# Softmax attention in a fused two-layer kernel: who empties v and the sums of values, and where the output projections are summed

## What is computed

```python
def _L0_attn_a_ref(x, Wq, Wk, Wv, Wo):          # 16 heads of 16
    q, k, v = (heads(x @ W.T) for W in (Wq, Wk, Wv))
    att = jnp.einsum('bhqd,bhkd->bhqk', q, k) / jnp.sqrt(16)
    p = jax.nn.softmax(att, axis=-1)
    out = jnp.einsum('bhqk,bhkd->bhqd', p, v)
    return merge(out) @ Wo.T

def _L1_attn_b_ref(x, W_q, Wd_kv, W_uv, W_uk, W_o, gamma, beta):   # latent keys and values, causal
    c_kv = _layernorm(x @ Wd_kv.T, gamma, beta)                    # 64 wide
    scores = einsum(q, absorbed_k, c_kv) / np.sqrt(16)             # masked above the diagonal
    v_full = heads(c_kv @ W_uv.T)
    ctx = einsum(softmax(scores), v_full)
    return merge(ctx) @ W_o.T

x = x + _L0_attn_a_ref(_layernorm(x), ...)      # layer 1, "MHA" below
x = x + ...                                     # layers 2 to 6: experts, linear attentions, experts
x = x + _L1_attn_b_ref(_layernorm(x), ...)      # layer 7, "MLA" below
x = x + _L1_ffn_ref(_layernorm(x), ...)         # layer 8
```

## Time and profile before

| | us |
|---|---|
| median of 3 runs (3069.28 to 3079.09) | 3072.86 |
| the profiled execution | 3071.74 |
| its span, first to last instruction | 3070.0 |
| TensorE busy in it, share of the span | 2791.3, 91% |
| VectorE busy | 1616.8, 53% |
| ScalarE busy | 844.4, 28% |
| GpSimd busy | 996.4, 32% |
| mean granted TensorE clock | 0.924 |

### The profile page before, as it was taken

One profiled execution on the slowest core, in us unless ns is written; L12 is line 12 of the kernel. 1 busy time (PEld: TensorE's weight loads), 2 busy tenths in 40 slices (PEclk: granted clock), 3 DMA queues, 4 the chain that ended last, 5 costly groups with the idle time before them and its releaser, 6 DMA issues. The chain is left out here.

```text
span 3070.0 us, 45793 instructions
## 1 busy us (share of the span) xinstructions
PE 2791.3 (91%) x15592; PEld 1943.7 (63%) x15592; DVE 1616.8 (53%) x4517; ACT 844.4 (28%) x1372; POOL 996.4 (32%) x1109
## 2 busy tenths in 40 slices
PE   7999999999999999999978999999999658888876
PEld 3434448887656556788867888888887533443444
DVE  4566645555655647455534333333344566555556
ACT  2343344443111101344432222222222002222210
POOL 0000027766544435577741122222221011212211
PEclk8999999999999999999989999999998558888875
DMA  3000020000000000200000000000000000000000
GB/s 142 1 0 0 0 103 1 0 0 0 1 0 0 0 0 0 83 0 0 0 14 1 15 15 15 15 1 15 15 1 1 24 0 1 1 1 0 1 0 28
DMA packets 6289, 37.96 MB, mean 12 GB/s; under 512 B 273, under 2 KB 4369, under 8 KB 4497
## 3 DMA queue, kind: packets, MB, share of 16 engines
q1 hardware_dynamic: 6160, 36.34, 3.0%
HBM read 34.24 MB, written 2.10 MB: 12 GB/s over the span
## 5 line engine op out<-in xcount | busy, mean ns | idle before, releaser
L603 PE MATMUL banks<-back 32*128 32x512 f32 (+3 forms) x1088 | 363.9, 599 | 31.5 <-DVE back L613 22.3
L365 PE MATMUL banks<-moe_parts 128*128 128x512 f32 x1536 | 366.9, 394 | 16.8 <-POOL moe_parts L471 10.3
L830 ACT ACTIVATE back<-banks 128x1024 f32<-128x1024 f32 (+3 forms) x256 | 217.1, 863 | 457.8 <-PE banks L724 457.5
L365 PEld LDWEIGHTS banks<-moe_parts 128*128 128x128 f32 x1536 | 286.2, 190 | 79.7 <-issue 22.4
L1449 PE MATMUL banks<-lin_parts 128*128 128x512 f32 x1152 | 309.1, 414 | 19.3 <-DVE lin_parts L1705 15.5
L1640 DVE TENSOR_TENSOR ffn_pack<-banks,back 128x512 f32<-128x512 f32 x128 | 88.5, 692 | 393.7 <-PE banks L1462 393.6
L1449 PEld LDWEIGHTS banks<-lin_parts 128*128 128x128 f32 x1152 | 213.2, 194 | 78.2 <-issue 31.2
L724 PE MATMUL banks<-back 32*128 32x512 f32 (+3 forms) x1024 | 239.4, 577 | 20.2 <-DVE back L846 12.8
L603 PEld LDWEIGHTS banks<-back 32*128 32x128 f32 x1088 | 134.2, 197 | 186.3 <-DVE back L617 77.9
L1770 POOL TENSOR_TENSOR ffn_pack<-ffn_pack 128x256 f32<-128x256 f32 x112 | 82.6, 738 | 456.9 <-ACT ffn_pack L1603 455.5
L617 DVE TENSOR_REDUCE back<-banks 128x1 f32<-128x512 f32 x272 | 176.5, 687 | 80.3 <-PE banks L603 75.6
(11 more groups left out here) (234 smaller groups left out, 5154.6 us busy)
## 6 DMA issues: line engine op xcount, KB each, us to landing
back<-p_raw SPq DMA_DIRECT2D x8, 1024.0 KB, 4.8
back<-p SPq DMA_DIRECT2D x1, 7696.0 KB, 21.2
ffn_pack<-ffn SPq DMA_DIRECT2D x1, 6144.0 KB, 26.8
back<-p SPq DMA_DIRECT2D x1, 5152.0 KB, 15.1
back<-p SPq DMA_DIRECT2D x2, 1792.0 KB, 8.2
out<-x SPq DMA_DIRECT2D x1, 2048.0 KB, 7.5
x<-x_in SPq DMA_DIRECT2D x1, 1536.0 KB, 12.7
small_pack<-small SPq DMA_DIRECT2D x1, 619.0 KB, 5.0
```

The costliest lines, as they stand in the source:

```text
L365: mm = nc.tensor.matmul(bank[:], up[:, n % 2, a, which, kd, :], xp[:, b, kd, :], start=((a, b, kd) == (0, 0, 0)), stop=((a, b, kd) == (1, ...
L603: nc.tensor.matmul(bank[:, 0:n], qs[head_rows[j], hg, qi * P:(qi + 1) * P], ks[head_rows[j], hg, 0:n], start=True, stop=True).then_inc(D.f ...
L830: nc.scalar.activation(pt[:, (kt % 2) * 2 + pair, :, q0:T], two[:, :, q0:T], ACT.Exp, scale=0.25).then_inc(A.free.s, 2)
```

## The change

- v: each of the four tiles now has a bank of ring A, and ScalarE copies it into `v` (128 x 256 each), at the start of ScalarE's turn. VectorE's three copies go. TensorE's two waits behind the last v tile go; in their place the transposed scores wait for their own two banks, the first sums of values (in the second key tile) wait for the last v copy, and v tile 2 waits until both adds of the turn before are done (`y_free`), since the banks 2 and 3 hold y.
- Sums of values: ScalarE copies `os_`, behind `keep_qk`, where VectorE did behind `put_max`.
- y: tiles 0 and 1 are summed in bank 2, tiles 2 and 3 in bank 3, and no longer as uses of ring A. Only the first matmul into a bank has the start flag. VectorE makes two adds of 128 x 512, each after both of its tiles; two new semaphores (`y_full`, `y_free`) tie them. TensorE waits for the last `keep_qk` ahead of the first projection, not ahead of the third.

```diff
-V_TILES = ((0, 1), (2,), (3,))
+    y_banks = c.banks[2:4]
-    A.open(HG * (2 + NT * HJ) + NT)
-    D.open(KD + w.extra_uses + len(V_TILES) + HG * (max_uses + 2))
+    A.open(NT + HG * (2 + NT * HJ))
+    D.open(KD + w.extra_uses + HG * (max_uses + 2))
...
+                def v_tile(i):
+                    pe.wait_ge(A.free.s, A.may_fill(it))
+                    w.v(A.fill("v", i)[:, 0:DM], i).then_inc(A.full.s, 1)
...
                 def project(i, groups):
                     for hg in groups:
-                        mm = nc.tensor.matmul(A.banks[A.index["y", i] % 4][:, 0:DM],
+                        mm = nc.tensor.matmul(y_banks[i // 2][:, (i % 2) * DM:(i % 2 + 1) * DM],
                                               os_[:, hg, i * P:(i + 1) * P], w.wo[:, hg, :],
-                                              start=(hg == 0), stop=(hg == HG - 1))
+                                              start=(hg == 0 and i % 2 == 0), stop=(hg == HG - 1),
+                                              skip_group_check=True)
...
-                for tiles in V_TILES:
-                    v_tiles(tiles)
-                pe.wait_ge(D.free.s, D.released(it, "v", V_TILES[-1]))
-                pe.wait_ge(A.free.s, A.all_free(it))
+                for i in range(NT):
+                    if i == 2:
+                        pe.wait_ge(c.y_free.s, c.y_free.at(it, 0))
+                    v_tile(i)
...
+                        if (hg, kt) == (0, 1):
+                            pe.wait_ge(A.free.s, A.released(it, "v", NT - 1))
...
+                pe.wait_ge(A.free.s, A.released(it, "k", 1))
                 for i in range(NT):
-                    pe.wait_ge(A.free.s, A.may_fill(it))
-                    A.fill("y", i)
                     project(i, range(HG - 1))
                 turn_reciprocals(HG - 1)
                 pe.wait_ge(D.free.s, D.released(it, "reciprocals", HG - 1))
                 for i in range(NT):
-                    project(i, range(HG - 1, HG)).then_inc(A.full.s, 1)
-                pe.wait_ge(A.free.s, A.released(it, "k", 1))
+                    mm = project(i, range(HG - 1, HG))
+                    if i % 2:
+                        mm.then_inc(c.y_full.s, 1)
                 pe.wait_ge(D.free.s, D.released(it, "turn", 0))
+            pe.wait_ge(c.y_free.s, c.y_free.at(B, 0))
...
         def _(act):
             with act.Fori(0, B) as it:
+                for i in range(NT):
+                    act.wait_ge(A.full.s, A.may_read(it))
+                    bank = A.read("v", i)
+                    nc.scalar.activation(v[:, i, :, 1:1 + DH], bank[:, 0:DM].rearrange("p (h d) -> p h d", d=DH),
+                                         ACT.Identity).then_inc(A.free.s, 1)
...
                     keep_qk(act, it, (hg + 2) % HG)
+                    act.wait_ge(O.full.s, O.may_read(it))
+                    bank = O.read("o", hg)
+                    nc.scalar.activation(os_[:, hg, :], bank[:], ACT.Identity).then_inc(O.free.s, 1)
...
         def _(dve):
-                for tiles in V_TILES:
-                    keep_v(tiles)
...
-                    dve.wait_ge(O.full.s, O.may_read(it))
-                    bank = O.read("o", hg)
-                    nc.vector.tensor_copy(os_[:, hg, :], bank[:]).then_inc(O.free.s, 1)
                 invert(HG - 1)
                 normalise(HG - 1)
-                for i in range(NT):
-                    n = A.index["y", i]
-                    dve.wait_ge(A.full.s, A.full.at(it, n + 1))
-                    nc.vector.tensor_tensor(c.x[:, it, i, :], c.x[:, it, i, :], A.banks[n % 4][:, 0:DM], ALU.add)\
-                        .then_inc(A.free.s, 1)
+                for half in range(2):
+                    dve.wait_ge(c.y_full.s, c.y_full.at(it, half + 1))
+                    xs = c.x[:, it, 2 * half:2 * half + 2, :]
+                    nc.vector.tensor_tensor(xs, xs, y_banks[half].rearrange("p (a d) -> p a d", a=2), ALU.add)\
+                        .then_inc(c.y_free.s, 1)
```

More of the change, by code:

```diff
@@ L683, in _ @@
             pool.wait_ge(c.s_small.s, 16)
-            nc.gpsimd.memset(mp[:], 0.0)
+            nc.gpsimd.memset(mp[:], 0.0).then_inc(c.y_free.s, 1)
             if causal:
@@ L696, in softmax_attention @@
         c.kt_ready.close(1)
-    A.open(HG * (2 + NT * HJ) + NT)
-    D.open(KD + w.extra_uses + len(V_TILES) + HG * (max_uses + 2))
+    c.y_free.base += 1
+    c.y_full.open(2)
+    c.y_free.open(2)
+    A.open(NT + HG * (2 + NT * HJ))
+    D.open(KD + w.extra_uses + HG * (max_uses + 2))
     O.open(HG)
@@ L832, in _ @@
                     keep_qk(act, it, (hg + 2) % HG)
-                for i in range(NT):
-                    A.read("y", i)
+                    act.wait_ge(O.full.s, O.may_read(it))
+                    bank = O.read("o", hg)
+                    nc.scalar.activation(os_[:, hg, :], bank[:], ACT.Identity).then_inc(O.free.s, 1)
         @block.vector
@@ L840, in _ @@
                 norm = next_norm(nc, c, it)
[L842 to L848, removed]
                 def invert(hg):
@@ L925, in _ @@
                 spread(HG - 1)
-    for k in (A, D, O, c.xn_ready, c.max_ready, c.os_ready, c.ve):
+    for k in (A, D, O, c.xn_ready, c.max_ready, c.os_ready, c.y_full, c.y_free, c.ve):
         k.close()
@@ L2269, in program @@
         c.os_ready = Count(sem("os_ready"))
+        c.y_full = Count(sem("projected"))
+        c.y_free = Count(sem("projected_added"))
         c.s_x = Count(sem("s_x"))
```

## The result

The changed kernel takes 3034.86 us in the median (four runs, 3034.18 to 3037.58), the kernel before 3071.07 beside it: a ratio of 0.9897, interval 0.9874 to 0.992. The profiled execution took 3037.58 us, 34.2 less than the one of before.

A forecast was written before the change was run, and what follows sets the result against it. TensorE, busy 91% of the span, was taken as the bound, so only its waits counted. Gains of 2.8 + 8.9 + 1.6 - 0.5 = 12.8 us, 25.4 with the clock, plus 1.1 for the median, gave 3047 us; range 3041 to 3060.

The forecast's parts named there:

- MHA: 2.8 + 0.4 - 0.3: MHA loop: 2.8 us from the wait behind v, 0.4 from ScalarE's sums copies, 0.27 lost to the layer's longer last add.
- MLA without the clock: 8.9 + 1.2 - 0.3: MLA loop: 8.9 us from waits behind v, 1.2 from ScalarE's sums copies, 0.27 lost to the layer's longer last add.
- MLA's clock: Head group 0, MLA turns 1 to 3: with the 3 us waits cut, full clock and 16.2 us each, gaining 12.6 us.
- The wait behind v: Turn starts: TensorE's scores no longer wait for v's last copy, gaining 2.8 us in MHA and 8.9 in MLA.
- Sums of values: Turn ends: ScalarE's copy lets TensorE's denominators start 0.1 us earlier in MHA, 0.3 in MLA; 1.6 us over all turns.
- The pair of tiles in a bank: Turn ends, y: sharing a bank loses no overlap, since only the last add decides; the skill's rule would cost 3.4 us.
- the clock didn't fall: Rival, MLA turns 1 to 3: the clock falls all the same, time 3060 us; chance 0.19 for falling in all.
- the wait didn't change hands: Rival, turn starts: the wait only changes hands, to the second score pair, VectorE's return and `y_free`; 3051 us, chance 0.12.
- no pause ahead of an exponential: Sign on ScalarE: idle "issue" time ahead of an exponential would prove the prediction wrong; VectorE's pause at its jump was 2.73 us.

The follow-up runs named there:

- the run with the 0.5 us stage: Changed kernel with an extra stage between layers 1 and 2 in which VectorE writes 128x128 zeros, so later layers start 0.5 us later: 3036.59 us, ratio 0.9898.
- The delayed start: Changed kernel with an extra stage between layers 1 and 2, four VectorE writes of 128x512 zeros taking 2.6 us: 3045.32 us, ratio 0.9928; layer 3 took 515.3 us.

## Why the prediction came out as it did

By the terms of its sum, profiled execution against profiled execution:

| term | predicted, us | measured, us | from |
|---|---|---|---|
| MHA: 2.8 + 0.4 - 0.3 | 2.9 | 3.0 | the loop's windows |
| MLA without the clock: 8.9 + 1.2 - 0.3 | 9.8 | 7.8 | the rest of MLA's 20.3 |
| MLA's clock | 12.6 | 12.5 | 423.8 before less 413.6 with the wait filled, and 2.3 that the filling itself costs |
| layers not touched | none | 10.9 | layers 3 and 5 |

*The wait behind v: right,* in size and in its reason. Scores follow v at once; VectorE's pause stays (2.38 us, seen in the run with the wait put back) and lies beside TensorE's work; `y_free` holds tile 2 for 0.37 us where I had 0.2 to 0.3.

*The clock: right, in size too.* Head group 0 gave what was forecast (16.2 us in turns 1 to 3 with the wait filled, from 19.3, 19.3 and 22.6), and the loop bears it out, 12.5 us. What MLA as a whole lacks, 20.3 us against 22.4, lies in turn 0: the low stretch out of the prologue, which the kernel before didn't have there. Without it, in the run with the 0.5 us stage, head group 0 of turn 0 and the loop read

```profile
2538.34:2554.54 16.20, 14.63 (x101) 6.13 (x102) 11.24 (x65) 6.43 (x12) 4.38 (x16) 1.00 0.01 2
2534.60:2934.80 400.20, 345.71 (x2144) 168.99 (x2144) 219.12 (x1076) 121.69 (x192) 86.46 (x272) 0.90 0.00 1
```

and the loop is 23.6 us under 423.8. The forecast for MLA lies between the two.

*Sums of values: right in sign, the size in MLA not shown.* TensorE's wait at the turn's end fell by 0.10 us in MHA and 0.31 in MLA, the 0.1 and 0.3 that I had. Alone this part showed 0.3 us in MHA's loop, where I had 0.4; MLA's 0.4 us, where I had 1.2, are within its variation, and the median shows nothing.

*The pair of tiles in a bank:* worth nothing that can be seen, as the rows said.

*The step that failed* is that the sum ends at the two attentions. I took every other layer at its length of before. Layer 3 begins 3.1 us earlier, by MHA's gain alone, and this takes its four waits of 3.02 us to where the clock doesn't fall behind the first three of them: 7.5 us in the profile. The delayed start brings 5.9 of them back, and the filled waits give the whole to the kernel before with the attentions as they were, 9.3 us in the median. The changed kernel gains less by the same filling, 0.4 to 2.8 us by the times and 3 to 6 by the ratios, so some 4 to 9 us between the medians are layer 3's. That the shift hit upon a better place and not a worse one was luck: the run with the latents' wait filled lost it again. The trace of before showed what was needed for a bound: a wait of 3.02 us at each turn start of layer 3 and matmuls at 1.2 GHz behind it. I had priced the clock where the change cuts a wait, and not where it only shifts one. With layer 3's bound of 8.4 us (516.9 less 508.5) the range would have reached to about 3033. The 3.4 us in layer 5 aren't the change's: two executions of the kernel before differ by 3.8 us there. A smaller part of the miss is the 1.1 us that I added for the median: the changed kernel's median lies 2.7 us under its profiled execution.

The rivals: the clock didn't fall behind the cut waits in the two profiles, the wait didn't change hands, and ScalarE's loop of 48 instructions shows no pause ahead of an exponential (its first one in a turn, [0.73 <-PE], waits for scores). Whether it pauses at its own jump isn't shown: in the changed kernel it waits for v there.

## What to carry to other kernels

A change that moves everything behind it by a few microseconds can change layers that it doesn't touch, where TensorE waits with the clock near a fall; look for such waits in the trace of before and let the range hold what they cost. Ask of a wait what it costs in the stage behind it too: filling one with work of no use showed that in one run, and kept the clock. Take what the filling itself costs out of the reading, here 2.3 us in the turn whose wait was short. Compare layer by layer before a gain is credited to the edit.

## What the runs showed of the hardware

- A wait's length alone doesn't tell whether the clock falls. Behind the first wait of 3.02 us in layer 3 it fell in one kernel and held in the other; behind 1.31 us it fell, and the group behind took 20.4 us instead of 16.2; behind 0.69 us it held.
- Matmuls of no use, 5.4 us of them in a turn, shortened a loop of four turns by 10 to 13 us (390.5 us against 400.1 to 403.5), because most of the low clock behind an idle TensorE went away: over the loop the clock rose from 0.89 to 0.96.
- What sets, within an execution, the times at which the clock falls wasn't found. That layer 3's length steps from 509.4 to 516.9 us between starts at 743.0 and 743.5 us is what these executions show, one each.
